# A decoder's narrow-head attentions: the next item's front in a walk of its own

## The reference

```python
# L0_xattn (block 1): squared relu in place of softmax
scores = jnp.einsum('bqhd,bshd->bhqs', rq, rk) / sqrt(ADIM)
scores = jnp.where(mask[:, None, :, :], jnp.float32(-1e+32), scores)
t = jax.nn.relu(scores + nbias[0]); t = t * t
attn = t / (t.sum(-1, keepdims=True) + IEPS)
# L1_xattn (block 4): relative positions by a shifted second product
ac = jnp.einsum('bhtd,bhsd->bhts', qh + b_u[None, :, None, :], kh)
bd = left_shift(jnp.einsum('bhtd,hmd->bhtm', qh + b_v[None, :, None, :], ph))
attn = jax.nn.softmax(jnp.where(mask, (ac + bd) / math.sqrt(D_K), -jnp.inf), axis=-1)
# L2_attn (6): window of 64 by softmax; L2_xattn (7): masked softmax;
# L3_attn (9): 4 key heads for 16, q and k normalised and rotated, causal window of 64
```

## Time and profile before

| | |
|---|---|
| median of 3 runs | 2542.19 us (2542.02 to 2546.29) |
| the profiled execution: its time, and its span | 2545.29 us, 2543.0 us |
| PE busy | 2107.1 us, 83% |
| DVE, ACT, POOL busy | 57%, 47%, 7% |
| mean granted clock of TensorE | 0.917 of 2.4 GHz |
| instructions | 41734 |

### The profile page before, as it was taken

How to read it: one execution, slowest core, us unless ns; L and a number is a source line. 1 busy time by engine, 2 the same in 40 slices (tenths; PEclk the granted TensorE clock), 3 DMA queues, 4 the chain that set the end, 5 groups by cost and what they waited for, 6 DMA issues and landing times.

```text
span 2543.0 us, 41734 instructions
## 1 busy us (share of the span) xinstructions
PE 2107.1 (83%) x15996; PEld 1619.2 (64%) x15996; DVE 1447.9 (57%) x4786; ACT 1189.9 (47%) x2876; POOL 180.4 (7%) x173
## 2 busy tenths in 40 slices
PE   7766999999957467589887788889998997689999
PEld 5544786666635344368775565557786885478898
DVE  5766417677755575576665555553343434556654
ACT  2455436656636466462142333335756674333222
POOL 3000000000000000000000000000001212210000
PEclk9888999999978798799998888889998998799999
DMA  5223000000037658641102322221011002120000
GB/s 190 69 72 96 2 1 1 1 1 1 1 103 203 167 159 229 164 114 67 26 22 97 77 57 56 60 60 31 2 30 26 26 22 54 44 57 21 12 5 7
DMA packets 170310, 154.91 MB, mean 61 GB/s; under 512 B 11113, under 2 KB 159105, under 8 KB 169473
## 3 DMA queue, kind: packets, MB, share of 16 engines
q1 hardware_dynamic: 170112, 152.25, 21.8%
HBM read 88.08 MB, written 63.34 MB: 60 GB/s over the span
## 4 chain that ended last, share of the span: by engine, by line
PE 55%; DVE 18%; ACT 11%; DMA 8%; issue 3%; POOL 3%; SPq 2%; DVEq 0%; ACTq 0%
PE banks L508 49%; ACT P L1201 5%; DVE P L1516 3%; ACT L1201 2%; DMA skew<-region 2%; SPq L2183 2%; PE banks L808 2%; POOL route L2156 2%; ACT kz L1201 2%; DVE negm L1527 2%; DVE P L1589 1%; DMA qs<-mpT 1%; PE banks L904 1%; DVE P L1747 1%; DMA stacks<-P 1%
## 5 line engine op out<-in xcount | busy, mean ns | idle before, releaser
L508 PE MATMUL banks<-xnT,region 128*128 128x256 f32 x1696 | 448.0, 394 | 22.6 <-DVE x L1516 7.9
L508 PEld LDWEIGHTS banks<-xnT,region 128*128 128x128 f32 x1696 | 312.6, 196 | 75.1 <-ACT kz L1201 15.1
L1201 ACT ACTIVATE P<-banks 128x512 f32<-128x512 f32 (+3 forms) x432 | 198.7, 499 | 242.2 <-PE banks L508 217.2
L1201 ACT ACTIVATE P<-P,negm 128x256 f32<-128x256 f32 x512 | 253.7, 498 | 96.9 <-DVE negm L1767 69.6
L508 PE MATMUL banks<-region,kz 128*128 128x128 f32 x2304 | 282.3, 276 | 9.6 <-ACT kz L1201 4.9
L508 PEld LDWEIGHTS banks<-region,kz 128*128 128x128 f32 x2304 | 276.2, 192 | 20.5 <-ACT kz L1201 6.3
L508 PE MATMUL banks<-qs,kz 128*128 128x256 bf16 (+2 forms) x1024 | 228.2, 267 | 54.6 <-issue 21.9
L1201 ACT ACTIVATE kz<-banks,perm 128x256 f32<-128x256 f32 x400 | 166.1, 472 | 225.6 <-PE banks L508 224.6
L508 PE MATMUL banks<-kz,qs 128*128 128x256 bf16 (+1 forms) x768 | 188.0, 281 | 29.7 <-DVE negm L1527 15.7
L2108 POOL TENSOR_TENSOR rstd<-rstd,pows 128x2 f32<-128x2 f32 x96 | 68.3, 711 | 2015.4 <-DVE rstd L1520 2015.3
L1524 DVE SCALAR_TENSOR_TENSOR x<-banks,w,x 128x128 f32<-128x128 f32 x256 | 77.9, 346 | 210.0 <-PE banks L508 207.0
(11 more groups left out here) (225 smaller groups left out, 3811.5 us busy)
## 6 DMA issues: line engine op xcount, KB each, us to landing
stacks<-P SPq DMA_DIRECT2D x160, 192.0 KB, 3.1
skew<-region SPq DMA_DIRECT2D x64, 256.0 KB, 3.0
qs<-stacks SPq DMA_DIRECT2D x40, 384.0 KB
kz<-stacks SPq DMA_DIRECT2D x80, 192.0 KB, 3.4
skew<-region SPq DMA_DIRECT2D x64, 128.0 KB, 2.6
skew_room<-skew SPq DMA_DIRECT2D x32, 256.0 KB, 3.2
P<-skew SPq DMA_DIRECT2D x32, 256.0 KB, 3.5
ctxT<-in_ctxT SPq DMA_DIRECT2D x32, 128.0 KB, 2.1
```

What stands on the lines that cost most here:

```text
L508: return p.e.matmul(o, lhsT, rhs, start=start, stop=stop)
L1201: return a.e.activation(o, i, f, **kw)
```

## The change

Every engine gets a walk for each stream that holds the fronts of the narrow-head blocks: on TensorE, ScalarE and SyncE a new one, on VectorE and GpSimd the walk that had the norms. A front may go one item ahead of the attention that uses it. For that:

- second rooms for items of odd number: `v_of`, `qs_of` (the room `qv`, unused outside L1_xattn), `qv_of`, `maskT_of`, `mask_of`; pieces and natural copies lie in rooms of their own (`pieces_of`, `natural_q`, `natural_k`, `natural_qv`);
- `kz` becomes two rooms of keys without zeros (`ks_of`): even heads at partitions 0 to 47, odd heads at 64 to 111 (`PAR` = 64), and the same for `qs`, `qv` and the positions (`ph`). The products contract 48 rows, or 51 with the three rows of maxima of each parity (`AUG` = 51). `clean_heads` and `zero_rows` are gone; the rows of ones are written once, by GpSimd;
- the front uses one bank, T (S1 in L1_xattn), in turn for the transposed norm, for q and k in its halves, and for the values. The attention weighs into V alone, which ScalarE empties twice an item instead of once. `finish` turns the output in V (in S0 in L1_xattn);
- the first front of a block waits for the stream's previous block (`x_done`) except in L2_xattn, which follows on; in L1_xattn a front waits until the 16 shifts of the item before are out;
- context and masks are loaded when the previous front is done with them;
- `TURNS` is another order for all five engines.

```diff
-                        mm(o, s.kz[:, par, i, k * 128:(k + 1) * 128], s.qs[:, i, q0:q0 + n], True, False)
+                        mm(o, ks[r:r + rows, i, k * 128:(k + 1) * 128], qs[r:r + rows, i, q0:q0 + n], True, False)
                         m = mm(o, identb[:, :], mask_t[:, k, q0:q0 + n], False, True)
...
-                    i = mm(s.S1[:, t * S + far:(t + 1) * S], s.qv[:, h // 2, t * 128:(t + 1) * 128], phz[:, h % 2, h // 2, far:])
+                    i = mm(s.S1[:, t * S + far:(t + 1) * S], qv[r:r + HALF, h // 2, t * 128:(t + 1) * 128], ph[r:r + HALF, h // 2, far:])
...
+        def front_norm(s, j, bank):
+            m = FRONT_SEQ.index(j)
+            yield
+            p.wait_ge(s.xn_ready, j + 1)
+            if j % ITEMS == 0 and j != 7 * ITEMS:
+                p.wait_ge(s.x_done, j)
+            elif j // ITEMS == 4:
+                p.wait_ge(s.shift_out, H * (j % ITEMS))
+            p.wait_ge(s.f_out, 2 * m)
+            p.wait_ge(s.q_out, m)
+            p.wait_ge(s.k_out, m)
+            turned_item(s, j, bank).then_inc(s.f_full, 1)
+
+        def front(k_bank, wq, wk, wv, bias=None, loaded=None):
+            def run(s, b, j):
+                m, bank = FRONT_SEQ.index(j), s.bank[k_bank]
+                yield from front_norm(s, j, bank)
+                yield
+                p.wait_ge(s.f_out, 2 * m + 1)
...
+                mm(bank[:, 0:S], wq, s.xnT[:, :])
...
+                mm(bank[:, S:2 * S], wk, src).then_inc(s.f_full, 1)
+                yield
+                p.wait_ge(s.q_out, m + 1)
+                p.wait_ge(s.k_out, m + 1)
+                p.wait_ge(bias_sem, 48)
+                for t in range(TOK):
+                    o = bank[:, t * 128:(t + 1) * 128]
+                    i = mm(o, src[:, t * 128:(t + 1) * 128], wv, True, bias is None)
...
+        def stacks_in(s, j):
+            yield
+            p.wait_ge(s.stack_in, stacked(j) + 32 * stacks_of(j))
+            p.wait_ge(s.f_out, 2 * FRONT_SEQ.index(j) + 2)
...
         def L0_xattn(s, b, j):
-            yield from norm(s, j)
-            yield
-            yield from narrow_heads(s, W1["L0x_q"], W1["L0x_k"], s.xnT[:, :], s.ctxT[:, :])
-            yield from values(s, W1["L0x_v"], s.ctxT[:, :], None)
-            yield
-            yield from stacked(s)
-            p.clear(s, "T")
-            yield from attend(s, s.maskT, True)
+            yield from stacks_in(s, j)
+            p.wait_ge(s.mask_ready, j % ITEMS + 1)
+            yield from attend(s, j, s.maskT_of[j % 2], True)
```

More of the change, by code:

```diff
@@ L940, in L1_xattn @@
             p.clear(s, "V")
[L941 removed]
+            yield from finish(s, j, W1["L1x_o"], None, ("T", "V"), ("S0", 0))
         def route(s, gate, bias):
@@ L1103, in L2_xattn @@
-            yield from values(s, P["L2x_v"], s.ctxT[:, :], RW["L2x_vb"])
-            yield
-            yield from stacked(s)
-            yield from score_maxima(s, s.mask, 0, S)
-            yield from put_maxima(s)
-            yield from attend(s, s.maskT)
-            yield from finish(s, j, P["L2x_o"], RW["L2x_ob"], clear=True)
-        def L3_attn(s, b, j):
-            yield from norm(s, j)
-            yield
+            yield from stacks_in(s, j)
+            p.wait_ge(s.mask_ready, ITEMS + j % ITEMS + 1)
@@ new lines, in front_rope, with L3_attn @@
+            p.wait_ge(s.qk_ready, j % ITEMS + 1)
+            for k, a in enumerate((qn, kn)):
+                for t in range(TOK):
+                    i = p.e.transpose(bank[:, k * S + t * 128:k * S + (t + 1) * 128], a[:, t, :], ident)
+            i.then_inc(s.f_full, 1)
+        def L3_attn(s, b, j):
+            yield from stacks_in(s, j)
+            p.wait_ge(s.q_out, FRONT_SEQ.index(j) + 1)
+            p.wait_ge(s.k_out, FRONT_SEQ.index(j) + 1)
+            yield from attend(s, j, bands[:, 4:6, :], False, 64, 192)
@@ L1300, in L0_xattn @@
                 a.wait_ge(rel_out_sem, 16)
-            yield from norm(s)
-            yield
-            yield from narrow_heads(s, None)
-            yield from values(s)
-            yield
             yield from attend(s, ACT.Relu)
-            yield from finish(s)
+            yield from finish(s, s.V)
         def L0_ffn(s, b, j):
@@ L2415, in sync_program @@
                 dma(s.skew[k // 2, k % 2, :, S:2 * S].rearrange("(t p) m -> p t m", p=128), zeros, skew_zero)
-        alternate(d, [L0_attn, L0_xattn, idle(5), L1_attn, L1_xattn, L1_ffn, L2_attn, L2_xattn, idle(27), L3_attn, L3_xattn, L3_ffn])
+        alternate(d, [L0_attn, idle(1), idle(1), L1_attn, L1_xattn, L1_ffn, L2, L2, idle(1), idle(1), L3_xattn, L3_ffn],
+                  [no_front, front, no_front, no_front, front, no_front, front, front, no_front, front, no_front, no_front])
         d.wait_ge(out_sem, 16 * B)
```

829 lines of the change are left out of this document (403 added, 426 removed).

## The result

The changed kernel takes 2867.52 us (median of 4 runs, 2863.36 to 2901.87) against 2542.44 us before: ratio 1.1304, interval 1.1217 to 1.1392, so 13% slower. Forecast were 2580 us and at most 2650. The profiled execution took 2869.68 us with a span of 2867.9 us, 325 us more than before.

A forecast was written before the change was run, and what follows sets the result against it. PE (TensorE) was taken as the bound, with 336 us idle in four stretches against 365 us of shape changes. Terms -3 - 3 - 49 + 80 + 20 - 8 = +37 on 2545.3 gave 2582, forecast 2580 us, range 2465 to 2650.

The forecast's parts named there:

- the clock over 0.95: Sign expected in the new profile of the whole kernel: a granted clock over 0.95, beside a PE share over 90%.
- a PE need: PE time per item in each stage, counted from steps such as 0.11 us (256 bf16 columns) and 0.07 (160).
- Cost of a change: At score and shift products: 0.095 us per change of array shape, 3840 changes, 365 us of PE at full clock.
- The upper bound of 0.19: Upper estimate in us for each change of shape, twice 0.095, should the clock stand at its lower level.
- L2_attn, forecast 60 per item: L2_attn's item time: PE need 56.6 us with changes, over 0.94 gives 60 for 50.2 before.
- L2_xattn, 74 forecast: L2_xattn's item time: PE need 69.6 us with changes, over 0.94 gives 74 for 63.2 before.
- The term for it: L0_xattn: items 43.7 us for 48.6, first item 41 instead of 27.7; about -3 us with the tail.
- L1_xattn, 81 per item forecast: L1_xattn's item time, 81 us for 96 before (between 75 and 90); with the context load, -49 us.
- L2 was to bring +100 and L3 -8: L2: +80 us for stream 0's items, +20 for stream 1's beside dense experts; L3_attn: -8 us.
- tight packing: Rival for all stages: same cost of changes, but PE filled to 0.98 and L1_xattn at 75 us; 2510 us, chance 24%.
- The change of shape costs nothing: Rival: 48 rows run as the full array or row halves overlap; 2315 us, with stalls up to 2420, chance 11%.
- The front stays exposed: Rival: a front's DMA in SP's queue or a bank wait holds up the other stream or PE; about 2660, chance 8%.

The follow-up runs named there:

- full_rows: The changed kernel, its score, shift and maxima products contracting 96 (99) rows from partition 0, so scores sum two heads; 2352.86 us, ratio 0.924.
- the bench: Two separate programs on TensorE alone, stretches of 400 bf16 products of 256 columns in various row counts and mixes; steps of 0.054 to 0.325 us.
- snake: The changed kernel with both score products of a head together, then both masks, odd heads doing masks first; 2511.8 us, ratio 0.9875 to the kernel before.
- pairs: The changed kernel with both heads' four score products alternating between row halves and two banks, then four masks; 2575.43 us, ratio 1.0123 to the kernel before.

## Why the prediction failed

**The step that failed is the clock**: "the clock over 0.95" and a PE need counted from steps at the full clock throughout. In its place the runs show 0.807, and 0.51 in L2_attn. The direction was right, the size off by 288 us, 37 forecast and 325 measured in the span.

By parts, in medians: the walks alone were priced at 2315 and measured at 2353 (full_rows), 38 of the 288. The narrow rows were to add 265 (2580 less 2315) and added 515, the other 250. The changes themselves fit that forecast: an estimated 357 us of PE's time (worked out below), and PE's idle time shrank by 89, from 288 us in full_rows to 199, which leaves 268. The rest, about 247 us, is the clock's share.

- *Cost of a change, 0.095 us: right to a tenth.* It is 0.10 to 0.11 in the timeline of the changed kernel and 0.105 in the bench. The count was somewhat high, 3840 against 3464, and the two errors nearly cancel: 365 us forecast, 357 found. The upper bound of 0.19 "should the clock stand at its lower level" was wrong: there 48 and 128 in turn take 0.325, which is 0.212 for the product and 0.113 for the change. What doubles is the product, and no term of the sum priced that.
- *The two costs in the sum.* Between full_rows and the changed kernel PE's busy time differs by 599.8 us. My count over the two traces gives 3464 more changes, 357 us at 0.103. The other 243 us go with some 857 us more at the lower clock (1107 less 250, by the mean clocks), 0.28 us lost for each. That share fits the steps: from 0.17 to 0.245 us with 160 columns is 0.31 of the time. The traces bear the split out, as both kernels issue the same 15996 products in the same order and can be laid side by side. At 1258 places with a new change, both at the full clock, the steps (without waits) are 118 us longer (0.094 each); at 356 places, both at the lower clock, 40 us (0.112 each); at 1828 places where the clock is now the lower one too, 341 us (0.19 each); and at some 2500 places without a new change where only the clock is lower, 125 us. All other places together give -24 us.
- *L2_attn, forecast 60 per item, measured 87 in one stream and 92 in the other.* At the measured step both streams' 256 score and mask products take 256 x 0.245 = 62.7 us; the other 2 x (3.0 + 4.2) double to 28.8. Together 91.5, an estimate. The counts of the prediction were about right and the clock wrong.
- *L2_xattn, 74 forecast, 94.7 measured,* at a clock of 0.69: the same, in part.
- *L0_xattn.* The last item ended at 281.6 before and at 314.0 after: 32 later where -3 was forecast. The items take 48.2 at a clock of 0.78, not 43.7, and the first one ends 34 us later, not 13; in full_rows it ends 14 later (141.1). The term for it starts from 35.1 us, which the prediction doesn't work out.
- *L1_xattn, 81 per item forecast, 88.2 measured, 80.2 in full_rows.* Its chain of transfers was judged rightly. It is the one of these four stages where an item became clearly shorter. From the last item of L0_xattn to that of L1_xattn the time fell by 28, of 49 forecast.
- *From there to the end*, +321 us (rounded parts of the table above: 186, 78 and 56) where L2 was to bring +100 and L3 -8. This is 229 of the missing 288. In L3_attn the clock is 0.81 too. The 56 behind it had no term in the sum.
- *Packing.* The rival "tight packing" was to decide from a PE use of 0.96. The use did go there, 0.99 in L2, and the time came out above every forecast: a busy share says nothing of the speed at which PE is busy.
- *"The change of shape costs nothing"* priced the walks alone at 2315, up to 2420 with stalls. full_rows is that kernel, 2353. Its stretches are -30, -59 and -97 where that rival had -32, -66 and -129. For the first two that is a gain worked out well. In the third it is partly luck: up to the last item of L2_xattn full_rows gains 159 where -84 was forecast, and behind it loses 62 where -45 was.
- *"The front stays exposed"* fell: the stack DMAs go out amid the attention, and PE idles 199 us in all, 436 before. (Its own terms add up to about 2650, not 2660.)

What misled: the stages before had clocks of 0.82 to 0.89 with idle time beside them, and I put the low clock down to the idle time, so a filled PE had to mean a full clock. The Trainium skill reads the same way: the page "TensorE: Matmul & The Clock Gate", Part 1, lets activity release the throttle and ties the level to how busy the PE has been. The traces here disagree for narrow products: 361 us busy of 366 at 0.51 in L2_attn, and 48 rows alone without a gap at 0.50 in the bench. The Trainium skill's page "TensorEngine Tiling (Array Packing)", Key Properties, says that a switch of the tiling mode drains the engine. The bench fits that, with 0.105 us for a switch and a border between 64 and 80 rows. The doubled speed that the section Theoretical Speedup of the same page of the Trainium skill promises for at most 64 rows is there as well (0.054 us side by side), but pairs, the one use of it here, lost more by its wait for two banks.

Left open: a version with the new walks, wide rows and the parities apart. It needs zeros in one operand beside the second rooms, and no run shows whether there is room for them; in the bench products with zeros in 80 of 128 rows lost neither step nor clock. Nor was it tried to bring back L2_attn's clock in snake. How many rows, and in which order with full products, the clock bears is known only for the mixes of the bench. Why the last stretch of the new walks is 56 us longer was not tested.

## What to carry to other kernels

Cutting a contraction from 128 rows with zeros to 48 saved nothing (0.11 us either way at the full clock) and, alternated with full products, cost twice: about 0.1 us at every crossing, and the clock. Before filling an engine's idle time, read the granted clock beside its busy share, and look at the order in which shapes alternate. Where narrow products can't be avoided, put like beside like across neighbouring groups. That took the same work from 2868 to 2512 us.

## What was not expected of the hardware

PE can be busy 99% of 366 us at a granted clock of 0.51. In the bench 48-row products with no gap between them ran at half the clock. 64 rows alone kept it; 64 rows in turn with 128 did not. 80 and 96 rows beside 128 cost 0.003 us a step. 128-row products with zeros in 80 of the rows ran as full ones do (0.108 us, clock 1.00). And the cost of a change hardly grows at the lower clock (0.113 against 0.105 us).
